# Second layer of a four-layer graph network: radial matmuls in two row groups of 64 partitions, bias as bf16 parts, and the sums of three of eight portions as identity matmuls

## What is computed

```
R = relu(w * w1 + b1) @ w2 + b2            # w: the edge's weight; 64 hidden, 384 columns after a rearrangement
Y = spherical_harmonics(edge_attr_3)       # 9 values
msg[u, o] = sum over v, f, i of  R[u, v, k] * Y[f] * C[o, f, i] * x[src][v, i]   # 8 scalars and 8 vectors
out = zeros.at[dst].add(msg)               # sum over the edges of a node
x = layernorm(x + out)
```

## Time and profile before

| | us |
|---|---|
| median of 3 runs | 18546.1 |
| lowest, highest | 18534.44, 18557.52 |
| span of the profiled execution, from its first to its last instruction | 20972.7 |
| second layer in it | 6640 to 12480 |

### The profile page before, as it was taken

The page is one execution under the profiler, slowest core; times in us unless marked ns, Lnnn a source line. Parts: engine busy times, 40 slices in busy tenths (PEclk is TensorE's granted clock), DMA queues, the critical chain, the costliest instruction groups (busy, mean ns, idle before and its releaser), DMA issues. The chain is left out here.

```text
span 20972.7 us, 293199 instructions
## 1 busy us (share of the span) xinstructions
PE 13068.2 (62%) x92471; PEld 7362.5 (35%) x92471; DVE 11202.5 (53%) x19689; ACT 3071.4 (15%) x5120; POOL 11778.5 (56%) x10055
## 2 busy tenths in 40 slices
PE   0565555555554676776766652555555555699999
PEld 0344434333333444444444431122222112355554
DVE  2565544444444777777777773333332222567777
ACT  0222222222221111111111110111111111000000
POOL 4788888888886555555555554666666665100000
PEclk6565555555556888888888885666666666799999
DMA  7333333333333222222222213333333343489998
GB/s 276 47 39 37 37 39 39 39 37 37 38 39 46 47 49 47 48 47 47 48 46 48 46 40 35 73 70 72 76 71 71 71 76 63 125 257 293 292 293 267
DMA packets 2998639, 1817.14 MB, mean 87 GB/s; under 512 B 1730466, under 2 KB 2755819, under 8 KB 2979019
## 3 DMA queue, kind: packets, MB, share of 16 engines
q1 hardware_dynamic: 2201756, 1336.87, 25.1%
q0 software_dynamic: 669312, 166.80, 11.3%
q10 hardware_dynamic: 126512, 300.38, 4.1%
HBM read 1474.43 MB, written 392.90 MB: 89 GB/s over the span
## 5 line engine op out<-in xcount | busy, mean ns | idle before, releaser
L2005 POOL DMA_INDIRECT xg<-d_tab,s_i x3136 | 3254.6, 1038 | 2615.5 <-POOLq L1996 1630.7
L2537 POOL DMA_INDIRECT xg<-d_tab,s_i x3136 | 2996.6, 956 | 1865.8 <-issue 954.8
L2265 PE MATMUL pR<-w,H 128*128 128x384 f32 x6272 | 2703.4, 560 | 1407.6 <-PEq L2259 834.5
L1403 POOL DMA_INDIRECT d_acc<-AG,ix x1568 | 2471.5, 1576 | 527.2 <-issue 459.5
L1403 POOL DMA_INDIRECT d_acc<-T,ix x1568 | 2466.3, 1573 | 478.3 <-issue 437.1
L2923 PE MATMUL pacc<-nodes,HB 128*32 128x512 fp8e4 x47040 | 2663.0, 380 | 42.7 <-PEq L2967 42.7
L2574 DVE TENSOR_TENSOR_SCAN U<-mU,U,up 128x512 f32<-128x512 f32 x392 | 501.6, 1280 | 3289.0 <-DVEq L2573 2688.6
L2265 PEld LDWEIGHTS pR<-w,H 128*128 128x128 f32 x6272 | 1225.8, 215 | 2533.1 <-issue 2182.8
L2695 PE MATMUL hb<-U,Wbc 128*128 128x512 f32 x784 | 642.4, 914 | 2204.7 <-PEq L2691 2023.1
L1756 PE MATMUL pm<-ms,eq 128*128 128x32 f32 x6272 | 1366.4, 399 | 890.5 <-PEq L1754 888.8
L2923 PEld LDWEIGHTS pacc<-nodes,HB 128*32 128x32 f16 x47040 | 1261.5, 97 | 1317.1 <-issue 57.1
(11 more groups left out here) (338 smaller groups left out, 17504.3 us busy)
## 6 DMA issues: line engine op xcount, KB each, us to landing
packed<-d_A SPq DMA_DIRECT2D x420, 1792.0 KB
row<-d_m SPq DMA_DIRECT2D x1568, 64.0 KB
xg<-d_tab,s_i POOLq DMA_INDIRECT x6272
wrow<-d_w SPq DMA_DIRECT2D x196, 512.0 KB
d_scan<-so ACTq DMA_DIRECT2D x392, 256.0 KB
d_A<-stage ACTq DMA_DIRECT2D x97, 784.0 KB
d_ea<-in_ea_t ACTq DMA_DIRECT2D x1, 50176.0 KB
d_exp<-T ACTq DMA_DIRECT2D x1, 50176.0 KB, 250.4
```

The lines of the kernel that those rows point to most:

```text
L1403: e.indirect_dma_start(out=d_acc[i], out_offset=bass.IndirectOffsetOnAxis(ap=ix[k][:, t:t + 1], axis=0), in_=mo[k][:, t * F:(t + 1) * F], ...
L2005: e.indirect_dma_start(out=xg[k][:, t, :], out_offset=None, in_=d_tab, in_offset=bass.IndirectOffsetOnAxis(ap=s_i[n][:, t:t + 1], axis=0)) ...
L2265: last = e.matmul(pR[u % 2][:, j, 0:384], H[k][:, (2 * u + j) * P:(2 * u + j + 1) * P], w2[:, :], start=True, stop=True)
L2537: e.indirect_dma_start(out=xg[n][:, j * ST + c, :], out_offset=None, in_=d_tab, in_offset=bass.IndirectOffsetOnAxis(ap=s_i[d][:, col:col + ...
```

## The change

For each portion u the two matmuls now have the edge columns u and u + 8. H holds the hidden values of columns 0 to 7 in partitions 0 to 63 and those of 8 to 15 in partitions 64 to 127, w2 stands in both halves, and each matmul has K = 64 in its own half. The bias comes from a bf16 matmul ahead of each: a tile of ones against b2s, whose first three rows of each half hold the bias as a sum of three bf16 parts. Portion 2 joins the identity sums, which are now 192 columns wide and all stand behind portion 4; the turn is one piece ahead of portion 5.

```diff
-            wrow = [sb(st, f"wrow{n}", [64, GE]) for n in range(DEEP)]
-            H = [sb(st, f"H{k}", [P, GE]) for k in range(2)]
+            wrow = [sb(st, f"wrow{n}", [P, GE // 2]) for n in range(DEEP)]
+            H = [sb(st, f"H{k}", [P, GE // 2]) for k in range(2)]
...
-            PP = sb(st, "PP", [P, 2, 2, 16, F])
+            PP = sb(st, "PP", [P, 3, 2, 16, F])
...
-            pQ = ps(edges, "pQ", [P, 4, F])
+            pQ = ps(edges, "pQ", [P, 3, 2, F])
...
-                        e.dma_start(wrow[n][:, :].rearrange("h (c n) -> h c n", c=ST), bc(w_v[:, bass.ds(s * SW, SW)], 0, 64)
-                                    ).then_inc(S(f"w{n}"), 16)
+                        for h in range(2):
+                            e.dma_start(wrow[n][64 * h:64 * h + 64, :].rearrange("h (c n) -> h c n", c=2),
+                                        bc(w_v[2 * h:2 * h + 2, bass.ds(s * SW, SW)], 0, 64)).then_inc(S(f"w{n}"), 16)
...
+                    for h in range(2):
+                        for i in range(3):
+                            row = 64 * h + i
+                            e.dma_start(b2s[row:row + 1, :], b2p[i][row:row + 1, :]).then_inc(S("lb"), 16)
...
+                    for i in range(3):
+                        e.tensor_copy(b2p[i][:, :], b2t[0][:, :]).then_inc(S("vc"), 1)
...
+                            e.tensor_tensor(b2t[0][:, :], b2t[0][:, :], b2p[i][:, :], ALU.subtract).then_inc(S("vc"), 1)
...
-                        j, t = u % 2, slice(2 * u, 2 * u + 2)
+                        j, t = u % 2, slice(u, T, 8)
...
-                        if u < 2:
+                        if u < 3:
                             to = PP[:, u, :, :, :]
...
-                            if u > 4:
+                            if u > 5:
                                 e.wait_ge(S("vq"), 1)
...
-                            if u > 2:
+                            if u > 3:
                                 sums(k, u - 1)
...
-                        e.activation(H[k][0:64, :], wrow[n][:, :], ACT.Relu, bias=b1c[:, 0:1],
+                        e.activation(H[k][:, :], wrow[n][:, :], ACT.Relu, bias=b1c[:, 0:1],
                                      scale=w1c[:, 0:1]).then_inc(S(f"H{k}"), 1)
...
-                        e.activation(FX[k][:, :, :, 0:8], turned[:, 1:3, :, :].rearrange("p o t v -> p t o v"), ACT.Copy
-                                     ).then_inc(S("ca"), 1)
+                        for h in range(2):
+                            e.activation(FX[k][:, :, h, :, 0:8],
+                                         turned[:, 1:3, 8 * h:8 * h + 8, :].rearrange("p o u v -> p u o v"), ACT.Copy
+                                         ).then_inc(S("ca"), 1)
...
-                        e.activation(Q[k][:, :, 0:4, :].rearrange("p r t u -> p t r u"),
-                                     pQ[:, :, :].rearrange("p t (r u) -> p t r u", u=8), ACT.Copy).then_inc(S("qc"), 1)
+                        for h in range(2):
+                            e.activation(Q[k][:, :, 8 * h:8 * h + 3, :].rearrange("p r t u -> p t r u"),
+                                         pQ[:, :, h, :].rearrange("p t (r u) -> p t r u", u=8), ACT.Copy
+                                         ).then_inc(S("qc"), 1)
...
                             hidden((n + 2) % 4)
+                            spread((n + 2) % 4)
                             early_sums((n + 1) % 2)
-                            spread((n + 2) % 4)
...
-                        freed = "PP" if u in (2, 3) else "fpR"
+                        freed = "PP" if u in (2, 3, 4) else "fpR"
...
                         for j in range(2):
-                            last = e.matmul(pR[u % 2][:, j, 0:384], H[k][:, (2 * u + j) * P:(2 * u + j + 1) * P], w2[:, :],
-                                            start=True, stop=True)
+                            half = slice(64 * j, 64 * j + 64)
+                            e.matmul(pR[u % 2][:, j, 0:384], onesr[half, :], b2s[half, :], start=True, stop=False)
+                        for j in range(2):
+                            half = slice(64 * j, 64 * j + 64)
+                            last = e.matmul(pR[u % 2][:, j, 0:384], H[k][half, u * P:(u + 1) * P], w2[half, :],
+                                            start=False, stop=True)
...
                         radial(n, 2, past)
                         radial(n, 3, past)
-                        early_sums(0, 8)
                         radial(n, 4, past)
-                        early_sums(8, 16)
+                        early_sums(0, 6)
+                        if not last:
+                            turn(0, 3)
+                        radial(n, 5, past)
                         if past:
                             columns((n + 3) % 4)
-                        radial(n, 5, past)
-                        if not last:
-                            turn(0, 1)
+                        early_sums(6, 11)
                         radial(n, 6, past)
-                        if not last:
-                            turn(1, 3)
+                        early_sums(11, 16)
                         radial(n, 7, past)
```

More of the change, by code:

```diff
@@ L1906, in gnn_kernel @@
             w2 = sb(st, "w2", [P, 384])
[L1907 to L1911, removed]
+            w2t = [sb(st, f"w2t{n}", [P, 384]) for n in range(3)]
+            b2t = [sb(st, f"b2t{n}", [P, 384]) for n in range(4)]
+            b2p = [sb(st, f"b2p{n}", [P, 384], BF16) for n in range(3)]
+            b2s = sb(st, "b2s", [P, 384], BF16)
+            onesr = sb(st, "onesr", [P, P], BF16)
+            w1c = sb(st, "w1c", [P, 1])
+            b1c = sb(st, "b1c", [P, 1])
             FG = [sb(st, f"FG{k}", [P, T, 16]) for k in range(2)]
-            FX = [sb(st, f"FX{k}", [P, T, 2, 16]) for k in range(2)]
+            FX = [sb(st, f"FX{k}", [P, T // 2, 2, 2, 16]) for k in range(2)]
             hp = sb(st, "hp", [P, 3, 3, T, 8])
@@ L1964, in load @@
                                     d_fr[bass.ds(s + 4, 1), :, :].rearrange("a p x -> (a p) x")).then_inc(S(f"le{n}"), 16)
-                    for n in range(3):
-                        load(0, n, sources=False)
+                    load(0, 0, sources=False)
+                    load(0, 1, sources=False)
+                    e.wait_ge(S("bp"), 1)
+                    e.sem_inc(S("bp"), -1)
+                    for h in range(2):
+                        for i in range(3):
+                            row = 64 * h + i
+                            e.dma_start(b2s[row:row + 1, :], b2p[i][row:row + 1, :]).then_inc(S("lb"), 16)
+                    load(0, 2, sources=False)
                     with e.Fori(0, G // 4 - 1) as it:
@@ L2025, in _ @@
                 def _(e):
-                    for k in range(2):
-                        e.memset(H[k][64:P, :], 1.0).then_inc(S("vc"), 1)
+                    e.memset(onesr[:, :], 1.0).then_inc(S("vz"), 1)
+                    e.memset(b2s[:, :], 0.0).then_inc(S("vz"), 1)
+                    e.wait_ge(S("ld"), 192)
+                    e.sem_inc(S("ld"), -192)
+                    e.tensor_tensor(b2t[0][:, :], b2t[0][:, :], b2t[2][:, :], ALU.mult).then_inc(S("vc"), 1)
+                    e.tensor_tensor(b2t[1][:, :], b2t[1][:, :], b2t[3][:, :], ALU.mult).then_inc(S("vc"), 1)
@@ L2214, in _ @@
                     hidden(1)
+                    spread(1)
                     early_sums(0)
-                    spread(1)
                     with e.Fori(0, G // 4 - 1) as it:
```

79 lines of the change are left out of this document (42 added, 37 removed).

## The result

| | us |
|---|---|
| before, median of 20 runs | 18546.45 (18529.81 to 18557.52) |
| after, median of 20 runs | 18734.58 (18507.75 to 18745.44) |
| ratio after / before | 1.0067, interval 1.0041 to 1.0093 |
| span of the profiled execution after | 18733.6 |

The account below looks back on a forecast made before the run. VectorE was taken as the bound, 21.6 us a step; 19.25 + 3 radials of 1.3 gave 23.15, + 1.55 over 196 steps, + 304, taken as + 280 on 18546: 18,825 (18,700 to 18,950; whole range 18,430 to 19,330).

Parts of the forecast that it names:

- the radial portion at 1.3: TensorE's bias and main matmuls of one portion: 1.3 us, against 1.33 before, with only the middle two passes overlapping.
- rival (2): Full overlap of TensorE's row groups: a portion of 0.83, step 21.7, about 18,570 us, within 0.2%; chance 0.12.
- the ring: Closed path, TensorE from portion 2's products to portion 6's, then VectorE back: 19.25 + 3 radials, 23.15 us a step.
- the step before: One step of the kernel before, running freely: 21.6 us, set by VectorE, with slack on TensorE.
- DVE's own work: VectorE's work a step: 1.06 us less as portion 2 leaves its reduction, giving 20.5 us.
- P5 and P6: VectorE's products of portions 5 and 6, ahead of which it was to wait 2.6 us a step.
- 7.25 + 3 radials: TensorE's work in us from the end of portion 2's products to the start of portion 6's, radials at 1.3.
- the lower bound: Least time of a radial portion on TensorE, bias matmuls paired and both halves fully side by side: 0.83 us.
- Order on TensorE: All sums and the one-piece turn stand behind portion 4 on TensorE: + 1.55 us a step, + 304, taken as + 280.
- POOL's 21.4: GpSimd's 16 gathers a step, 1.04 busy and 0.3 issue each: 21.4 us, just below VectorE's 21.6, unchanged.
- Sums pass, crossings: On TensorE, 0.165 us a sums pass and 0.09 at each crossing between row groups and 128-row work, four on the path.
- Cheap edits: Activation, copies, earlier buffers: nothing; weights row in two transfers: nothing, at most 1 us a step; setup: + 5 us once.

Follow-up runs that it names:

- e1_fill: The kernel after with portions 2 and 3 computed twice into the same tile: 18267.16 us, ratio 0.9867 to the kernel before.
- e13_fill_one: The kernel after with only portion 3 computed twice: 18328.92 us, ratio 0.9884 to the kernel before.
- e8_sbuf_op: The kernel before plus one unused VectorE operation a step with both inputs in SBUF (0.56 us): 18644.80 us, ratio 1.0053.
- e11_split: The kernel before with the 512 KB weights row loaded by two transfers of 256 KB to the same 64 partitions: 18481.99 us, ratio 0.9966.
- e7_early_turn: The kernel before with the turn in one piece ahead of portion 5 and the spread earlier: 18583.27 us, ratio 1.0018.
- e0_before: The kernel before, unedited, profiled a second time, without holes: 18530.25 us, span 18528.1.
- e9_psum_op: The kernel before plus one unused VectorE operation a step that reads portion 3's PSUM tile (0.60 us): 18578.56 us, ratio 1.0016.
- e12_late_only: The kernel after with half of the sums and a third of the turn behind portion 6, no filler: 18238.26 us, ratio 0.9834.

## Why the prediction was right in direction and wrong in size

Three terms of the sum were mis-sized: the radial portion at 1.3, with rival (2)'s full overlap rated too low; the half clock in the ring, which had no term; and the step before, taken as VectorE's free 21.6. The runs show 0.83 at full clock (0.92 with a crossing), + 2.39 us, and 22.89. All that follows is for the upper group of the kernel after.

*DVE's own work: right.* Busy time a step is 3587.89 / 3800 x 22.89 = 21.61 before and 3282.70 / 3800 x 23.89 = 20.64 after, 0.97 less, for 1.06 predicted.

*The ring: right in its structure.* VectorE waits ahead of P5 and P6, 2.53 and 0.71, together 3.24 where the prediction had 2.6; TensorE has no idle time in between. From P6 to the end of P2 VectorE needs 12.0 (the steps repeat, so P6 stands 23.89 ahead of 9054.15, at 9030.26, and the tail behind P2 begins at 9042.26): exactly the predicted 12.0.

*TensorE's side of the ring: two terms mis-sized, with opposite sign.* The prediction had 7.25 + 3 radials. From P2's end (9042.26) to P6 (9054.15) it took 11.89:

| | predicted | after | e1_fill, full clock |
|---|---|---|---|
| start of portion 4 | in the 0.5 | 0.23 | 0.23 |
| portion 4 | 1.3 + 0.09 | 1.72 | 0.91 |
| sums 0 to 6 | 2.0 + 0.09 | 3.64 | 2.06 |
| turn | 2.0 + 0.09 | 2.03 | 2.03 |
| portion 5 | 1.3 | 0.92 | 0.91 |
| transposes | 0.44 + 0.3 | 0.49 | 0.49 |
| sums 6 to 11 | 1.65 + 0.09 | 1.72 | 1.72 |
| portion 6, to VectorE's start | 1.3 + the rest of 0.5 | 1.14 | 1.15 |
| sum | 11.15 | 11.89 | 9.50 |

(The last column is from e1_fill's own timelines, from the tail behind P2 at 9040.76 to P6 at 9050.26.)

*The radial term.* The prediction took 1.3 because the queue holds A1 A2 B1 B2 and it let only A2 and B1 meet. The records show otherwise: at full clock the two bias matmuls start 3 to 6 ns apart, 0.16 to 0.17 later two passes, 3 to 18 ns apart, and 0.32 after those two more. Four passes end within 0.81, and the portion costs the 0.83 of the lower bound and a crossing. That was rival (2)'s reading, rated 0.12, and the prediction had named passes that start together as a sign that it was wrong. The Trainium skill, "TensorE: Matmul & The Clock Gate", section "Part 3: Packing small matmuls", has starts about 4 ns apart in distinct row groups; the trace agrees with 3 to 6 ns for the bias matmuls and, less closely, with 3 to 18 for the fp32 passes. The prediction let the page's other half, program order, overrule it. In the trace starts are in order, but in pairs: two slots of 0.32 for four passes, not three. That each pair is one pass of either half is inferred; a record doesn't name its partitions.

*The clock.* The sum had no term for it. The faster radials leave TensorE busy for 3.9 of the 7.2 us between the starts of P1 and P4, and then portion 4 and the first sums meet the half clock: 0.81 + 1.58 = 2.39 us in a ring with no slack. It is the step "Order on TensorE" that failed to ask at which clock the jobs would run; the earlier trace rows with 0.86 gave the hint, and the prediction weighed a low clock only for the kernel before. e1_fill and e13_fill_one show the cause: the same jobs at full clock take 2.39 less, and the step follows the half clock when the filler changes it.

*The base.* "It has slack, so DVE is the bound of a step that runs freely" was 21.6 against a measured 22.89. POOL's 21.4 was mis-sized: the mean gather in the profile without holes is 1.055, and the time between two is 0.376 and not 0.3, since GpSimd also waits for the landing of earlier gathers (546.1 us of 3800). e8_sbuf_op and e11_split show that both parts weigh on the time; that nothing else bounds the step before is read from the trace's waits and was not shown by an experiment. The earlier trace rows had the first number nearly right and named such landings, 180.7 us, but the holes hid their weight behind 1556.2 us of L1996.

*The sum, with the measured terms.* Ring 12.0 + 9.5 = 21.5, half clock 2.39: 23.89. Less 22.89: + 1.00, x 196 = + 196, for 188 in the medians. The three errors are - 1.65 (radials and hand-overs), + 2.39 (clock) and - 1.29 (base), together - 0.55 a step. That a sum wrong in three places came within 90 us of the median is luck: the errors happened to offset each other. Had the radial alone been right, the forecast would have been rival (2)'s "within 0.2%", and the direction missed.

*Sums pass, crossings: right.* A sums pass is 0.163 at full clock, for 0.165. Row groups after 128-row work start 0.258 behind the last sums pass instead of 0.163, and 128-row work 0.413 behind a portion's last pass instead of 0.322: 0.09 each, as priced.

*Cheap edits.* ScalarE's hidden activation fell to 1.23, hidden as said. The weights row by two transfers was priced at nothing to + 1.0 a step and e11_split shows - 61 us, 0.3 a step less, a side that was not given. Gathers' buffers free earlier were said not to help "while POOL isn't last". POOL was last, and still they were worth nothing: GpSimd waited only 9 us in 3800 for them, and e7_early_turn, which frees them earlier, was not faster.

## What to carry over

Before a step is priced as a sum, settle which engine sets the pace now by what each engine waits for, in a profile whose span equals the timed runs; a mean of free steps is a lower bound only. When packing makes TensorE's jobs shorter, look at the stretch where it becomes idle and ask what stands right behind it: work that meets the half clock there grows (here portion 4 from 0.91 to 1.72, the sums from 2.06 to 3.64), and it is cheap to move it out of the ring or, as in e13_fill_one, to fill the stretch. Parts of a change that are good or neutral alone can cost together, here - 86 and 0 against + 188, so run the parts. And look whether an edit removed what it was meant to remove, before its time is read as a verdict.

## What the runs showed of the hardware

*GpSimd's gathers are held by VectorE.* In e0_before a gather that starts beside a VectorE operation with both inputs in SBUF is longer than the usual 0.94: 0.91 in the mean beside L2106 (123 gathers), 0.54 beside L2101 (164), 0.33 beside L2112 (85), 0.24 beside the head L2058 (120). The 0.91 is more than L2106's own 0.54 us: where the head doesn't follow at once it is 0.41 (57 gathers), so the rest goes with the head right behind. Beside the products that read PSUM it is 0.02 to 0.08 beside L2072 and L2080, and 0.00 beside the reductions L2089 (717); the 0.38 beside the products L2080 just ahead of L2106 (59) can be that tail's, which starts while such a gather runs. One case of each, from the timelines of VectorE and GpSimd of e0_before:

```profile
9002.19 1.34 DVE L2101 TENSOR_TENSOR tv<-Q,e 128x1152 f32<-128x1152 f32 x1
...
9004.66 0.54 DVE L2106 TENSOR_TENSOR tv<-tv 128x384 f32<-128x384 f32 x1
```

```profile
9001.51 0.94 POOL L2005 DMA_INDIRECT xg<-d_tab,s_i  x1 [0.30 <-DMA xg<-d_tab,s_i]
9002.76 1.60 POOL L2005 DMA_INDIRECT xg<-d_tab,s_i  x1 [0.30 <-DMA xg<-d_tab,s_i]
9004.66 1.36 POOL L2005 DMA_INDIRECT xg<-d_tab,s_i  x1 [0.31 <-issue]
```

The Trainium skill, "SBUF — State Buffer", section "SBUF: two separate sides", says that a VectorE operation with two SBUF inputs and a GpSimd operation that reads SBUF exclude each other for the whole instruction; the trace agrees for the issue of an indirect DMA, with up to 0.66 and 0.42 in the rows above, and e8_sbuf_op against e9_psum_op shows its price in time.

*Two transfers for one.* Splitting a 512 KB load into two of 256 KB shortened the waits for gathers of another queue by 140 us in 3800, and the kernel by 61. Whether size or count does it is open.

Open stay also what puts a run of the kernel after into the lower or the upper group, and why e12_late_only meets the half clock in one step of four only.
